# Norms of a diffusion transformer: a shorter root, scaled rows signalled by tile, an early exponential

## What is computed

```python
x = x + block_a(ln(x), cond, ctx)     # self attention 16x64, cross attention on 77 rows, gated feed forward
x = x + block_b(ln(x))                # causal attention 16x64 with rotation, 31 routed experts and a shared one
x = x + block_c(ln(x), cond, ctx)     # six layers, below
x = x + block_d(ln(x))                # 64 routed experts and a shared one

def _ln(x, eps=1e-05):
    m = jnp.mean(x, axis=-1, keepdims=True)
    v = jnp.var(x, axis=-1, keepdims=True)
    return (x - m) * jax.lax.rsqrt(v + eps)

for i in range(6):                    # block_c: 16 heads of 8 columns
    xn = _adaln(x, cond, n1_w[i], n1_b[i])                     # _ln, then scale and shift by cond
    x = x + attn(rope(xn @ wq), rope(xn @ wk), xn @ wv) @ so_w[i].T
    xn = _adaln(x, cond, n2_w[i], n2_b[i])
    x = x + attn(rope(xn @ cq), rope(ctx @ ck), ctx @ cv) @ co_w[i].T
    xn = _adaln(x, cond, n3_w[i], n3_b[i])
    x = x + gelu(xn @ f1_w[i].T + f1_b[i]) @ f2_w[i].T + f2_b[i]
```

## Time and profile before

| | us |
|---|---|
| median of 3 runs (2586.89 to 2590.71) | 2590.1 |
| the profiled execution, its own time | 2589.37 |
| its span, first to last instruction | 2587.8 |

### The profile page before, as it was taken

One profiled execution on the slowest core, in us unless ns is written; L12 is line 12 of the kernel. 1 busy time (PEld: TensorE's weight loads), 2 busy tenths in 40 slices (PEclk: granted clock), 3 DMA queues, 4 the chain that ended last, 5 costly groups with the idle time before them and its releaser, 6 DMA issues.

```text
span 2587.8 us, 32244 instructions
## 1 busy us (share of the span) xinstructions
PE 2220.2 (86%) x11288; PEld 882.6 (34%) x11288; DVE 1693.5 (65%) x3937; ACT 1137.7 (44%) x1863; POOL 143.1 (6%) x143
## 2 busy tenths in 40 slices
PE   7999989889998897887887888788788878867898
PEld 3333333533333563223323222332322233232433
DVE  5766767645666678755775675577568557754464
ACT  3333333122223333663665566366546636644311
POOL 0000000011110210000000000000000000010000
PEclk9999999799999898897999799799979979988999
DMA  3000000300000110000100010010001000030000
GB/s 146 1 1 1 1 1 1 115 1 1 1 1 1 52 27 19 25 1 25 41 3 9 18 43 1 25 43 2 17 10 43 1 25 26 2 102 1 1 1 8
DMA packets 38032, 54.33 MB, mean 21 GB/s; under 512 B 5073, under 2 KB 34546, under 8 KB 36338
## 3 DMA queue, kind: packets, MB, share of 16 engines
q1 hardware_dynamic: 37874, 52.28, 6.4%
HBM read 32.34 MB, written 0.52 MB: 13 GB/s over the span
## 4 chain that ended last, share of the span: by engine, by line
PE 39%; DVE 10%; ACT 8%; issue 4%; SPq 1%; DMA 0%; ACTq 0%; DVEq 0%
PE ps L2116 7%; PE ps L2096 5%; ACT big L2601 4%; PE ps L2077 4%; DVE C_nm L2778 4%; PE ps L2244 2%; PE ps L2161 2%; PE ps L2351 2%; PE ps L2256 2%; PE ps L2347 2%; PE ps L2372 2%; PE ps L2263 2%; ACT big L2681 2%; PE ps L2272 2%; PE ps L2221 1%
## 5 line engine op out<-in xcount | busy, mean ns | idle before, releaser
L2778 DVE TENSOR_REDUCE C_nm<-ps 128x1 f32<-128x512 f32 x768 | 501.1, 684 | 183.4 <-PE ps L2077 179.1
L2601 ACT ACTIVATE big<-ps 128x512 f32<-128x512 f32 x768 | 427.9, 595 | 231.0 <-PE ps L2096 220.5
L2077 PE MATMUL ps<-C_attn 62*128 62x512 bf16 x768 | 275.1, 416 | 60.3 <-DVE C_nm L2778 52.0
L2096 PE MATMUL ps<-C_attn 64*128 64x512 bf16 x768 | 253.0, 396 | 63.1 <-ACT big L2601 52.5
L2116 PE MATMUL ps<-big,C_attn 128*32 128x512 f32 x1536 | 213.2, 628 | 13.3 <-ACT big L2601 13.3
L2077 PEld LDWEIGHTS ps<-C_attn 62*128 62x128 bf16 x768 | 63.2, 94 | 303.2 <-DVE C_nm L2778 165.9
L2096 PEld LDWEIGHTS ps<-C_attn 64*128 64x128 bf16 x768 | 59.3, 93 | 275.9 <-ACT big L2601 206.0
L2681 ACT ACTIVATE big<-ps,C_biasx 77x512 f32<-77x512 f32 x192 | 115.6, 679 | 58.0 <-PE ps L2248 57.9
L879 DVE TENSOR_REDUCE A_nm<-ps 128x2 f32<-128x1024 f32 x64 | 77.7, 1214 | 87.8 <-PE ps L609 87.5
L797 ACT ACTIVATE A_p<-ps 128x1024 f32<-128x1024 f32 x64 | 65.6, 1025 | 111.0 <-PE ps L637 110.8
L797 ACT ACTIVATE B_p<-ps 128x1024 f32<-128x1024 f32 (+1 forms) x64 | 45.0, 703 | 149.7 <-PE ps L641 149.7
(11 more groups left out here) (414 smaller groups left out, 3785.4 us busy)
## 6 DMA issues: line engine op xcount, KB each, us to landing
C_attn<-C_first SPq DMA_DIRECT2D x144, 128.0 KB, 2.4
C_w<-in_C_w SPq DMA_DIRECT2D x6, 1090.0 KB, 5.1
C_attn<-in_D_ew SPq DMA_DIRECT2D x4, 1536.0 KB, 10.6
big<-in_B_ew SPq DMA_DIRECT2D x8, 514.0 KB
normw_later<-in_norm_w SPq DMA_DIRECT2D x1, 2304.0 KB, 16.0
A_w<-in_A_w SPq DMA_DIRECT2D x2, 1024.0 KB, 11.6
A_w<-in_A_w SPq DMA_DIRECT2D x2, 768.0 KB, 8.8
B_w<-in_B_w SPq DMA_DIRECT2D x1, 1536.0 KB, 9.9
```

Of the source, the lines that this page charges most:

```text
L2077: pe.matmul(ps[:, bank, :], lhsT=qs[side(hp, MAX_ROW), b, 2 * q + pq, t * P:(t + 1) * P], rhs=ks[side(hp, MAX_ROW), b, 2 * q + pq, :], sta ...
L2096: pe.matmul(ps[:, bank, :], lhsT=ks[side(1 - hp, HALF), b, 2 * q + pq, kt * P:(kt + 1) * P], rhs=qs[side(1 - hp, HALF), b, 2 * q + pq, :], ...
L2601: act.activation(prob[:, kt % 2, pq, 1 - hp, :], ps[:, bank, :], ACT.Exp, scale=SCALE)\
L2778: dve.tensor_reduce(nm[:, q % 2, t, pq, hp:hp + 1], ps[:, bank, :], AX.X, ALU.max, negate=True).then_inc(emptied[bank], 1)
```

## The change

Three things change.

The root: `seed_steps` forms the magic number's difference in one instruction, by a factor of -0.5 on the bit pattern where a shift and a factor of -1 stood. `rstd_steps` has one Newton round of three instructions and one third-order round of four, where three Newton rounds stood. `Norm.root` keeps its three rounds.

The handover in the six layers: each of the four scalings in `apply` raises `xn_ready`, and `turn_norm` waits for each tile ahead of its transposition; the other waits on that semaphore count in fours. The wait for the bank now stands ahead of the wait for the rows.

The exponential: behind the fourth Gelu of batch 0 in the first five layers ScalarE runs an exponential of one column into a tile `early` that nothing reads.

```diff
--- before.py
+++ after.py
@@ -76,10 +76,14 @@
     seed_steps(c, dve, m, n, rms)
     y, t, u = m.rs[:, 0:n], m.lnt[:, 0:n], m.lnu[:, 0:n]
     v = m.lnv[:, 0:n]
-    for _ in range(3):
-        c.after(dve.tensor_tensor(t, y, y, ALU.mult))
-        c.after(dve.scalar_tensor_tensor(u, t, -0.5, v, ALU.mult, ALU.mult))
-        c.after(dve.scalar_tensor_tensor(y, u, 1.5, y, ALU.add, ALU.mult))
+    c.after(dve.tensor_tensor(t, y, y, ALU.mult))
+    c.after(dve.scalar_tensor_tensor(u, t, -0.5, v, ALU.mult, ALU.mult))
+    c.after(dve.scalar_tensor_tensor(y, u, 1.5, y, ALU.add, ALU.mult))
+    k = 0.375 ** 0.5
+    c.after(dve.tensor_tensor(t, y, y, ALU.mult))
+    c.after(dve.scalar_tensor_tensor(u, t, k, v, ALU.mult, ALU.mult))
+    c.after(dve.scalar_tensor_tensor(t, u, -1.25 / k, u, ALU.add, ALU.mult))
+    c.after(dve.scalar_tensor_tensor(y, t, 1.875, y, ALU.add, ALU.mult))
 
 
 def seed_steps(c, dve, m, n, rms):
@@ -92,8 +96,7 @@
         c.after(dve.scalar_tensor_tensor(v, t, EPS, var, ALU.add, ALU.add))
     else:
         c.after(dve.tensor_scalar(v, var, EPS, None, ALU.add))
-    c.after(dve.tensor_scalar(t.bitcast(I32), v.bitcast(I32), 1, None, ALU.arith_shift_right))
-    c.after(dve.tensor_scalar(y.bitcast(I32), t.bitcast(I32), -1.0, float(RSQRT_MAGIC), ALU.mult, ALU.add))
+    c.after(dve.tensor_scalar(y.bitcast(I32), v.bitcast(I32), -0.5, float(RSQRT_MAGIC), ALU.mult, ALU.add))
 
 
 def newton_steps(c, eng, m, n):
@@ -1983,6 +1986,7 @@
         probx = shared[0:CTX, :, :].rearrange("p (r g) s -> p r g s", r=2)
         cw, cwx = (m.pair[:, i * 2 * S:(i + 1) * 2 * S].rearrange("p (k s) -> p k s", s=S) for i in range(2))
         rden = sb("rden", [P, TB * QUAD])
+        early = sb("early", [P, 1])
         cn = m.cn[:].rearrange("p (b t d) -> p b t d", b=B, d=P)
         cT = sb("cT", [P, S])
         qx = sb("qx", [P, S])
@@ -2149,9 +2153,9 @@
                     last.then_inc(filled[bank], 1)
 
                 def turn_norm(key, b, count):
-                    pe.wait_ge(xn_ready, count)
                     bank = fill(key)
                     for t in range(TB):
+                        pe.wait_ge(xn_ready, TB * (count - 1) + t + 1)
                         last = pe.transpose(ps[:, bank, t * P:(t + 1) * P], m.xn[:, b * TB + t, :], m.ident[:])
                     last.then_inc(filled[bank], 1)
 
@@ -2547,13 +2551,13 @@
                         pool.tensor_tensor(parts[:, 1, 2, :], rem[:, 1, :], parts[:, 1, 1, :], ALU.subtract)\
                             .then_inc(k_p3, 1)
                     if s in at["VX"]:
-                        pool.wait_ge(xn_ready, norms(n, 1))
+                        pool.wait_ge(xn_ready, TB * norms(n, 1))
                         for k in range(2):
                             drained(pool, ("vx", b, k))
                         pool.tensor_copy(vx[:, b, :, 0:HD], cross.v[:, b, layer(n), :].rearrange("p (h d) -> p h d", d=HD))\
                             .then_inc(vx_ready, 1)
                     if s in at["BIAS"]:
-                        pool.wait_ge(xn_ready, norms(n, 2))
+                        pool.wait_ge(xn_ready, TB * norms(n, 2))
                         y = m.y[:, b * TB:(b + 1) * TB, :]
                         row = R_F2B + layer(n)
                         pool.tensor_tensor(y, y, m.rows[:, row:row + 1, :].broadcast_to([P, TB, P]), ALU.add)\
@@ -2691,6 +2695,8 @@
                         bank = arrived(act, ("ff", n, i))
                         act.activation(u[:, i, :], ps[:, bank, :], ACT.Gelu,
                                        bias=w[:, layer(n) % 2, LB1 + i:LB1 + i + 1]).then_inc(emptied[bank], 1)
+                        if i == 3 and b == 0 and n < UNITS - B:
+                            act.activation(early[:], m.ident[:, 0:1], ACT.Exp)
 
                 def tables_v(b):
                     if b == 0:
@@ -2752,7 +2758,7 @@
 
                 def stats(n, count):
                     if count > 1:
-                        dve.wait_ge(xn_ready, count - 1)
+                        dve.wait_ge(xn_ready, TB * (count - 1))
                     for t in range(TB):
                         ins = dve.bn_stats(m.st[:, t, :], m.y[:, n % B * TB + t, :])
                         c_.after(ins) if t == TB - 1 else c_.step(ins)
@@ -2768,9 +2774,7 @@
                         k = n % B * TB + t
                         ins = dve.tensor_scalar(m.xn[:, k, :], m.y[:, k, :], m.mv[:, t, 0:1], m.rs[:, t:t + 1],
                                                 ALU.subtract, ALU.mult)
-                        if t < TB - 1:
-                            c_.step(ins)
-                    ins.then_inc(xn_ready, 1)
+                        ins.then_inc(xn_ready, 1)
 
                 def row_max(n, i, hp):
                     q, pq, t = tile_of(i)
```

## The result

The changed kernel took 2564.8 us (median of four runs, 2563.0 to 2570.7) against 2590.4 of the kernel before on the same chip: ratio 0.990, interval 0.9881 to 0.992. That is 25.6 us less. The forecast was 2576 with a range of 2567 to 2584, so the sign was right and the size was not: the sum had given half of the gain.

A forecast was written before the change was run, and what follows sets the result against it. No engine bounds the kernel; only waits where all other engines stand still count. Layers 10.2, last layer 1.2, batch 1's norms 1.2 and opening 0.4 make 13.0 us off 2589.4, so 2576, range 2567 to 2584.

The forecast's parts named there:

- What bounds the kernel: Whole span: no engine fills it; an edit gains only where every other engine stands still, one place per layer.
- The root, 0.60 at each exposed norm: Norms TensorE waits for, between layers and outside: dropping the shift and two Newton steps saves 0.60 us each.
- Covered norms, nothing: The other 30 layer norms, beside attention: TensorE comes 0.87 us after the rows, so gain 0, at most 6 us.
- Rows tile by tile, 0.63: Batch 0's exposed norm, six times: transpositions run under the scalings, so ScalarE's copy starts 0.63 us earlier.
- The exponential, 0.81 between 0 and 1.30: Five cross attentions: table load moved into ScalarE's idle time; exponentials 1.30 us earlier, 0.81 us gained each.
- The sum, 13.0: Whole span: five layers 10.2, last layer 1.2, batch 1's two exposed norms 1.2, opening 0.4; together 13.0 us.
- The clock, which the sum leaves out: Half-clock dips, outside the sum: single dips coming or going put at 3 us either way over the span.
- a rival that made it longer: Half-clock stretch behind the norm grows: at half as long again 28 us lost, 2604; chance 0.05.
- The forecast's own last sign of being wrong: In the layers: the forecast is wrong if half-clock stretches change by several us a layer.
- I expect it to move and to stay: Half-clock dip behind batch 0's first norm: still there, moving with the work; if unmoved, 3.1 us lost in all.
- the clock stays up across the shorter wait: Behind the first norm between layers: the dip ends, 2.6 us a layer, 13 more, 2563; chance 0.08.
- The other rivals: Load not waited for or back, 2580.4, 0.10; attention swallows gains, 2586, 0.06; half-clock stretch grows, 2604, 0.05.

The follow-up runs named there:

- e1: Kernel before with the shorter root alone: seven Newton steps instead of nine and no shift; 2586.4 us, ratio 0.9988.
- e2: Kernel before with the scaled rows handed over tile by tile, alone; 2591.5 us, ratio 1.0.
- e3: Kernel before with the early one-column exponential alone; 2577.8 us, ratio 0.9944.
- d1: Kernel before with two more table loads ahead of the same five cross attentions; 2608.4 us against 2590.1, ratio 1.0052.
- the pair with fills: Changed kernel and kernel before, both with extra matmuls filling two TensorE waits per layer; means 2563.1 and 2582.3 us.
- e6: Changed kernel with extra matmuls in the waits for batch 0's first norm and ahead of batch 1's cross maxima; ratio 0.9888.

## Why the prediction was right or wrong

- **What bounds the kernel**: right. TensorE's wait on scaled rows fell from 31.1 to 24.1 us, and the steps of a layer changed in the exposed places and where half clock came or went.
- **The root, 0.60 at each exposed norm**: right, 0.60 to 0.62 in five layers (e1). The exposed norms outside, 0.60 each: 2.37 to 1.77, 6.48 to 5.90, 3.70 to 3.11. The last was worth 2.29 with the half clock that went with it.
- **Covered norms, nothing**: right. In the norm of the earlier trace rows the rows are now there at 1321.61 + 1.10 = 1322.71 and TensorE comes at 1324.19 (timeline after): 1.48 us behind them instead of 0.87, so the 0.6 went into cover.

```profile
1321.61 1.10 DVE L2775 TENSOR_SCALAR xn<-y,mv,rs 128x128 f32<-128x128 f32 x4
...
1324.19 0.66 PE L2159 MATMUL ps<-ident,xn 128*128 128x128 f32 x4
```

  The four transpositions take the same 0.66 us with their four waits as with one: the met waits cost nothing there.
- **Rows tile by tile, 0.63**: right, 0.64 to 0.65 (e2).
- **The exponential, 0.81 between 0 and 1.30**: right, 0.79 to 1.09 in four layers (e3). The Trainium skill ("ScalarE: Activation LUTs", section "What ACT_TABLE_LOAD costs") counts 2.66 us a switch. The trace doesn't agree: in d1 an activation follows 0.01 to 0.02 us behind each load of 1.28, and the next load 0.01 behind the activation.
- **The sum, 13.0**: right at one clock, 12.9 from ten runs, 13.9 from the pair with fills and 13.4 from two executions at the same clock. That the first comes within 0.1 is luck, with 0.8 of error and parts that do not add up.
- **The clock, which the sum leaves out**: this is the step that failed. "Single dips that come or go I put at 3 us either way over the span" was too small by far. The change met 0.0052 more mean clock, 8.4 us, over ten runs. The four runs of the first comparison had 0.0083 more than the mean of before; the same kernel's second set had 0.0035 more than before on its chip, so a part of the first 25.6 us was luck. The kernel before alone spreads over 25.6 us with its clock from run to run. The three runs on which the forecast rested (2586.9 to 2590.7) hid that, but its own trace did not: the stretch that lasts 27.3 us in four layers came out at 13.70 and 10.20 in the fifth. Half of it in five layers, at the 0.42 per us that I used for its growth, is 5 x 13.7 x 0.42 = 29 us, and still some 16 to 21 at the 0.24 to 0.31 that were measured. I gave that only to a rival that made it longer. The range should have carried it both ways. The forecast's own last sign of being wrong, half-clock stretches that change by several us a layer, is the one that came.
- **"I expect it to move and to stay"** (the dip behind the norm): half right. It stayed, at 4.43 us of idle time, but it moved with the work only in part, and the next step took back 2.6 us of the five gains, near the 3.1 that the prediction had named and set aside. In the sum at one clock this counts as clock.
- **The rival "the clock stays up across the shorter wait"** came near in time (2563), for the most part by another mechanism. At 4.43 us of waiting the clock fell as before; what got shorter were the later stretches. It came true at one place, the wait in the last experts: behind 3.70 us half clock came in all seven profiles with the old root, behind 3.11 us in three of the nine with the new one. Where it stayed away, the stretch to the end gained 2.3 us, otherwise at most 0.62.
- **The other rivals**: the loads are gone from the five places and none came back. The half-clock stretch that begins at 1201.8 did not grow beyond 27.4 us in any layer. The attention did not swallow the gains: the table's 0.81 is in its step.
- **What stays open**: why the long stretch was shorter in two layers of five; and why the early exponential goes with a higher clock while the waits are not filled (four pairs of four), and does not once they are. The stretches of one profile each can't tell it from chance.

The Trainium skill ("TensorE: Matmul & The Clock Gate", section "What's actually happening") says that how many matmuls at a kernel's start run at the lower clock varies from run to run, and puts the cost of that start under 1% of a typical kernel's span. No run here measures the start by itself. Over the whole span the mean clock varies too (0.925 to 0.938 in 72 runs), and the cost is larger. As an estimate from the runs' slope, carried far beyond their range: 357 us of half clock are 0.069 x 1610 = 111 us, 4% of this span.

## What to carry to other kernels

A sum of exposed waits held here to 0.02 us at the norms between layers, one place aside; make it from the one place where every other engine stands still, and give covered work nothing. Where the granted clock is below 1 in stretches that repeat, its change is a term of its own with a price and a range, also for an edit that doesn't touch TensorE. Compare two kernels at one mean clock, from many runs, before a part is called good or bad: alone, the handover here looked worthless and the exponential three times its worth. A gain right ahead of a half-clock stretch is not safe until the step behind it has been read as well.

## What the runs showed of the hardware

- One program, 72 runs on four chips, spread by 1% (2577.3 to 2602.9 us), and the time went with its mean granted clock, 1.73 us per 0.001.
- Behind a wait of 4.43 us the clock was at 0.50; with the same wait filled with matmuls it was 1.00, and half clock came later all the same: in e6 TensorE's row is busy 13.70 of 13.70 us at 0.50. Filling one wait was not enough to keep the clock up.
- The stretch at half clock behind a norm came 3.4 us sooner in the first layer when the work came 4.15 sooner, so more of the work fell into it (5.82 us of 6.80 instead of 4.65 in the third layer).
- Three table loads in a row, with a one-column activation of 0.20 us behind each of the first two, came to 4.30 us: nothing but 0.01 to 0.02 us stands between them beside the loads' 1.28 us.
